# Turning a normalised activation by VectorE blocks and a DRAM round trip instead of by TensorE

## The reference

```python
x = x + tanh(g_xattn[0]) * L0_xattn(layernorm(x), ctx, ...)      # stage A
x = x + tanh(g_ffn[0])   * L0_ffn(layernorm(x), ...)             # stage F
x = x + tanh(g_xattn[1]) * L1_xattn(layernorm(x), ctx, mask)     # stage L
x = x + tanh(g_ffn[1])   * L1_ffn(layernorm(x), ...)             # stage M

def L0_ffn(x, proj1, proj1_bias, proj2, proj2_bias, gate_w):     # hidden size 2048
    h = gelu(x @ proj1.T + proj1_bias)
    return h @ proj2.T + proj2_bias
```

## Time and profile before

| | us |
|---|---|
| median of 3 runs | 1939.48 (1938.37 to 1940.64) |
| profiled execution, its time | 1941.13 |
| profiled execution, its span | 1939.3 |

### The profile page before, as it was taken

The page is one execution under the profiler, slowest core; times in us unless marked ns, Lnnn a source line. Parts: engine busy times, 40 slices in busy tenths (PEclk is TensorE's granted clock), DMA queues, the critical chain, the costliest instruction groups (busy, mean ns, idle before and its releaser), DMA issues.

```text
span 1939.3 us, 25583 instructions
## 1 busy us (share of the span) xinstructions
PE 1900.6 (98%) x10102; PEld 962.7 (50%) x10102; DVE 1035.4 (53%) x2260; ACT 559.7 (29%) x873; POOL 280.7 (14%) x277
## 2 busy tenths in 40 slices
PE   6999998999999999999999999999999999999999
PEld 4556555644444444444444444444544444444444
DVE  7688866764545453443535545554555555545422
ACT  3145423422222221112212233232222333333321
POOL 3023211111102010101100011111111111111111
PEclk9999998999999999999999999999999999999999
DMA  6013322220101111110101020101010101000000
GB/s 218 12 42 124 106 89 82 87 98 17 44 28 60 28 64 50 56 55 22 62 1 55 1 71 1 50 1 50 1 50 1 50 1 45 5 11 13 1 22 22
DMA packets 56041, 86.99 MB, mean 45 GB/s; under 512 B 9042, under 2 KB 17362, under 8 KB 55922
## 3 DMA queue, kind: packets, MB, share of 16 engines
q1 hardware_dynamic: 55922, 85.36, 13.8%
HBM read 60.17 MB, written 25.17 MB: 44 GB/s over the span
## 4 chain that ended last, share of the span: by engine, by line
PE 86%; issue 8%; DVE 3%; POOL 1%; DMA 1%; ACT 1%; POOLq 0%; SPq 0%; DVEq 0%
PE bank L835 44%; PE bank L939 16%; PE bank L1033 10%; PE bank L844 5%; PE bank L919 4%; PE bank L885 1%; PE bank L904 1%; POOL arena L802 1%; PE bank L1020 1%; PE bank L968 1%; PE bank L995 0%; DMA x_after_ffn<-arena 0%; PE bank L984 0%; PE bank L983 0%; DMA arena<-x_after_attention 0%
## 5 line engine op out<-in xcount | busy, mean ns | idle before, releaser
L835 PE MATMUL bank<-arena 128*128 128x512 f16 x4608 | 1043.4, 380 | 3.1 <-DVE arena L1286 2.3
L835 PEld LDWEIGHTS bank<-arena 128*128 128x128 f16 x4608 | 451.0, 98 | 522.7 <-issue 5.5
L939 PE MATMUL bank<-arena 128*128 128x512 f16 x1536 | 352.1, 379 | 1.2 <-DVE arena L1469 1.2
L1033 PE MATMUL bank<-arena 128*128 128x512 f16 x1152 | 264.3, 379 | 0.9 <-POOL arena L802 0.9
L1621 DVE SCALAR_TENSOR_TENSOR arena<-bank,arena 128x512 f32<-128x512 f32 x96 | 72.0, 750 | 332.1 <-PE bank L835 332.1
L939 PEld LDWEIGHTS bank<-arena 128*128 128x128 f16 x1536 | 150.1, 98 | 173.9 <-DVE arena L1469 1.7
L1467 DVE TENSOR_SCALAR arena<-arena 128x512 f16<-128x512 f32 x128 | 69.4, 543 | 305.4 <-ACT arena L1134 305.2
L1134 ACT ACTIVATE arena<-bank,arena 128x512 f32<-128x512 f32 x128 | 99.6, 778 | 457.3 <-PE bank L835 454.3
L802 POOL TENSOR_TENSOR arena<-arena 128x512 f16<-128x512 f32 x96 | 111.1, 1157 | 628.7 <-ACT arena L1171 628.7
L844 PE MATMUL bank<-arena 128*128 128x128 f32 x1012 | 150.1, 279 | 26.4 <-DVE arena L1234 14.1
L1033 PEld LDWEIGHTS bank<-arena 128*128 128x128 f16 x1152 | 112.1, 98 | 128.3 <-POOL arena L802 1.4
(11 more groups left out here) (173 smaller groups left out, 1221.9 us busy)
## 6 DMA issues: line engine op xcount, KB each, us to landing
arena<-in_L_ffn_proj SPq DMA_DIRECT2D x48, 256.0 KB, 2.9
x_after_attention<-arena SPq DMA_DIRECT2D x8, 1024.0 KB, 4.7
arena<-x_after_attention SPq DMA_DIRECT2D x8, 1024.0 KB, 5.6
x_after_ffn<-arena SPq DMA_DIRECT2D x8, 1024.0 KB, 4.5
arena<-x_after_ffn SPq DMA_DIRECT2D x8, 1024.0 KB, 6.2
arena<-in_x SPq DMA_DIRECT2D x7, 1024.0 KB, 5.4
out<-arena SPq DMA_DIRECT2D x7, 1024.0 KB, 4.2
arena<-in_L_ffn_down_proj SPq DMA_DIRECT2D x48, 96.0 KB, 2.0
```

The source lines that it names most:

```text
L835: m = e.matmul(bank[b][:, :], wT[l][:, c, tile * P:(tile + 1) * P], y[h][:, c, :], start=n == 0, stop=n == NPASS - 1)
L939: m = e.matmul(bank[t][:, :], hv[h][:, 0, t * P:(t + 1) * P], w2T[l][:, j, :], start=j == 0 and i == 0, stop=j == NH - 1 and i == 2)
L1033: m = e.matmul(bank[t][:, :], hv[h][:, 0, t * P:(t + 1) * P], dnT[l][:, j, :], start=j == 0 and i == 0, stop=j == NR - 1 and i == 2)
```

## The change

In stage F, for batches 1 to 7 (`in_blocks`), the turned x is made in another way. `norm` is as before. VectorE then turns each 32x32 block of the 128x512 tile in place (`block`, into one of two new buffers `yb_s`), and SyncE stores the result to DRAM (`bstore`, 256 KB). When all four are there, four DMAs (`bload`) read them back, one for each 32 rows of the target, into a new fp32 buffer `yraw` with features on partitions; the runs in memory are 32 elements (128 bytes). Then ScalarE copies `yraw` to the high half in four pieces (`whole`), and GpSimd subtracts for the low half. `up` waits for these instead of for the turns. The task list for such a batch is that of `block_tasks`. The buffers lie above the old arena, which grows from 207 to 219 KB per partition. The line with `rate` isn't in the diff. Below, the three parts behind the DMAs are of GpSimd's, ScalarE's and VectorE's programs, in this order.

```diff
+def in_blocks(i):
+    ph, b = i
+    return ph == "F" and b > 0
...
     def ln_tasks(i, apart=False):
+        if in_blocks(i):
+            return block_tasks(i)
...
+    def block_tasks(i):
+
+        def stats():
+            for t in range(NT):
+                add("stat", i, t)
+            add("rs", i)
+
+        def step(t):
+            if t < NT:
+                add("norm", i, t)
+            if t > 0:
+                add("block", i, t - 1)
+                add("bstore", i, t - 1)
+
+        def whole(c):
+            add("whole", i, c)
+        return ([stats] + [lambda t=t: step(t) for t in range(NT + 1)] + [lambda: add("bload", i)]
+                + [lambda: None] * 6 + [lambda c=c: whole(c) for c in range(NC)])
...
+            elif kind == "bstore":
+                _, i, t = step
+                m = nth[step]
+                k = (nth["bload", i] - 1) % 2
+                w.wait_ge(b_ok, m)
+                if nth["bload", i] > 2:
+                    w.wait_ge(b_in, 64 * (nth["bload", i] - 2))
+                e.dma_start(yscr[k, t * P:(t + 1) * P, :], yb_s[(m - 1) % 2]).then_inc(b_out[(m - 1) % 2], 16)
+            elif kind == "bload":
+                _, i = step
+                m = nth[step]
+                k = (m - 1) % 2
+                w.wait_ge(b_out[0], 32 * m)
+                w.wait_ge(b_out[1], 32 * m)
+                if m > 1:
+                    w.wait_ge(b_lo, NC * (m - 1))
+                for q in range(4):
+                    rows = slice(q * 32, (q + 1) * 32)
+                    e.dma_start(yraw[rows, :, :].rearrange("r c (a s) -> r c a s", s=32),
+                                yscr[k].rearrange("(a r) (c q s) -> q r c a s", r=32, c=NC, q=4)[q]).then_inc(b_in, 16)
...
+            elif kind == "whole":
+                _, i, c = step
+                w.wait_ge(b_hi, n)
+                y_free(w, i)
+                hi, lo = y_of(i)
+                e.tensor_tensor(lo[:, c, :], yraw[:, c, :], hi[:, c, :], ALU.subtract).then_inc(b_lo)
...
+            elif kind == "whole":
+                _, i, c = step
+                w.wait_ge(b_in, 64 * nth["bload", i])
+                y_free(w, i)
+                e.activation(y_of(i)[0][:, c, :], yraw[:, c, :], ACT.Copy).then_inc(b_hi)
...
+            elif kind == "block":
+                _, i, t = step
+                m = nth["norm", i, t]
+                w.wait_ge(yn_ok, m)
+                if n > 2:
+                    w.wait_ge(b_out[(n - 1) % 2], 16 * ((n - 1) // 2))
+                e.transpose(yb_s[(n - 1) % 2], yn_s[(m - 1) % 2]).then_inc(b_ok)
```

More of the change, by code:

```diff
@@ L371, in build @@
 def build(nc, x_in, ctx_in, mask_in, gx_in, gf_in, wq, wg, bg, wkv, wo, w1, b1, w2, b2,
-          gw, gup, dnp, mg, dom, xa, xb, out, stack):
+          gw, gup, dnp, mg, dom, xa, xb, yscr, out, stack):
     plan = make_plan()
@@ L375, in build @@
     KB = 256
-    arena = stack.enter_context(nc.sbuf_tensor("arena", [P, 207 * KB], F32))
+    arena = stack.enter_context(nc.sbuf_tensor("arena", [P, 219 * KB], F32))
     def at(kb, words, dt=F32):
@@ L410, in build @@
     yn_s = [at(168 + 2 * i, D) for i in range(2)]
+    yb_s = [at(207 + 2 * i, D) for i in range(2)]
+    yraw = at(207 + 4, NC * TOK).rearrange("p (c n) -> p c n", c=NC)
     h_s = [at(172 + 2 * i, TOK) for i in range(2)]
@@ L498, in build @@
     y_turned, y_hi, y_lo = sem("y_turned"), sem("y_hi"), sem("y_lo")
+    b_ok, b_in, b_hi, b_lo = sem("b_ok"), sem("b_in"), sem("b_hi"), sem("b_lo")
+    b_out = [sem(f"b_out{i}") for i in range(2)]
     w_chain, w_rec, w_mx, w_zero, w_scaled = (sem(n) for n in ("w_chain", "w_rec", "w_mx", "w_zero", "w_scaled"))
@@ L634, in build, with y_ready @@
         w_landed[w] = landed[w % 4]
-    def y_rank(i):
-        return nth["turn", i, NT - 1]
+    def y_ready(w, i):
+        if in_blocks(i):
+            w.wait_ge(b_lo, nth["whole", i, NC - 1])
+        else:
+            w.wait_ge(y_lo, nth["turn", i, NT - 1])
     def bcast(v):
@@ L850, in tensor_program @@
                 w.wait_ge(const, C_ID)
-                w.wait_ge(yn_ok, n)
-                turn4(step, yn_s[(n - 1) % 2], y_turned)
+                m = nth[("norm", *step[1:])]
+                w.wait_ge(yn_ok, m)
+                turn4(step, yn_s[(m - 1) % 2], y_turned)
             elif kind == "wturn":
@@ L863, in tensor_program @@
                 _, b, j = step
-                w.wait_ge(y_lo, y_rank(("A", b)))
+                y_ready(w, ("A", b))
                 w.wait_ge(w_lo, n_lo["q"])
@@ L923, in tensor_program @@
                 _, b, j = step
-                w.wait_ge(y_lo, y_rank(("F", b)))
+                y_ready(w, ("F", b))
                 w.wait_ge(w_lo, n_lo["1"])
@@ L961, in tensor_program @@
                 v = bank[k][:, 0:NT * CTX].rearrange("p (t s) -> p t s", t=NT)
-                w.wait_ge(y_lo, y_rank(("L", b)))
+                y_ready(w, ("L", b))
                 w.wait_ge(c_copied, 2 * n)
@@ L988, in tensor_program @@
                 v = bank[k][:, 0:NT * NE].rearrange("p (t s) -> p t s", t=NT)
-                w.wait_ge(y_lo, y_rank(("M", b)))
+                y_ready(w, ("M", b))
                 w.wait_ge(w_lo, n_lo["gw"])
@@ L1054, in y_free @@
             w.wait_ge(sc_mm, b + 1)
+    yn_read = {nth[step]: (b_ok, nth[("block", *step[1:])]) if in_blocks(step[1]) else (y_turned, nth[("turn", *step[1:])])
+               for step in plan.steps if step[0] == "norm"}
     def y_of(i):
@@ L1232, in vector_program @@
                 if n > 2:
-                    w.wait_ge(y_turned, n - 2)
+                    w.wait_ge(*yn_read[n - 2])
                 e.tensor_scalar(yn_s[(n - 1) % 2], x[:, t, :], mv[:, t, 0:1], rs[:, t:t + 1], ALU.subtract,
@@ L1660 @@
     from concourse.bass_utils import run_bass_kernel_spmd
-    nc = bacc.Bacc("TRN2", target_bir_lowering=False, num_devices=1)
+    nc = bacc.Bacc("TRN2", target_bir_lowering=False, num_devices=1, dynamic_dma_scratch_size=1024)
     arrays, args = {}, []
@@ L1671 @@
     xb = nc.dram_tensor("x_after_ffn", (NB, TOK, D), F32, kind="Internal").ap()
+    yscr = nc.dram_tensor("normalised_blocks", (2, TOK, D), F32, kind="Internal").ap()
     out = nc.dram_tensor("out", (NB, TOK, D), F32, kind="ExternalOutput").ap()
     with ExitStack() as stack:
-        build(nc, *args, xa, xb, out, stack)
+        build(nc, *args, xa, xb, yscr, out, stack)
     r = run_bass_kernel_spmd(nc, [arrays], core_ids=[0])
```

## The result

| | us |
|---|---|
| before, median of 4 runs | 1939.74 (1938.37 to 1940.64) |
| after, median of 4 runs | 1954.11 (1953.82 to 1954.86) |
| ratio, with its 95% interval | 1.0075 (1.0063 to 1.0087) |
| after, profiled execution: time, span | 1953.82, 1952.0 |

The change costs 14.4 us. The forecast was 13.2 us, and 1954.11 us lies inside its range of 1942 to 1962.

The account below looks back on a forecast made before the run. TensorE, busy 98% of the span, was taken as the bound. Turns -12.2, wait -0.3, net stall +23.4 and clock +2.3 gave +13.2 us: 1952.7 us, with an 8-in-10 range of 1942 to 1962.

Parts of the forecast that it names:

- The large term: Batch 7, `down` (7,1) to `up` (7,4): 19 leftover weight calls issued without matmuls, net stall 23.4 us.
- What the removed turns give: TensorE, feed-forward batches 1 to 7: 28 transpose groups, 12.2 us, and one 0.31 us wait go; gain 12.5 us.
- What hides the added work: Beside TensorE: VectorE's block transposes (0.6 us each) and GpSimd's subtractions (1.16 us) were to cost nothing.
- The DMAs: Block loads of 8192 128-byte pieces per batch: 6 to 20 us to landing, 10 taken, at no cost.
- rival 3: 128-byte loads come too late for `up` 11's GELU, deciding from 27 us (53 ns per packet); about 2050 us; chance 0.11.
- The size of the stretch: Before `up` (7,4): SyncE's 50 down_proj DMAs, then the router's weight, delay it by 29.2 us.
- SyncE never waits: In batch 7's stretch, staging buffers free up before SyncE's issues need them, with the scale at about +9 us.
- rival 1: Batch 7's stretch is bound by the engines, not SyncE's issues: 19.9 us, +3.9 in all, 1943.4 us; chance 0.10.
- The clock: Behind batch 7's stretch: 4.6 us of matmuls at half speed, 2.3 us more, bounds 0 and 5.
- The sum: Whole kernel: -12.2 - 0.3 + 23.4 + 2.3 = +13.2 us, to 1952.7 us.
- net stall: Batch 7, before `up` (7,4): 29.2 us later, less 5.8 us of transposing done elsewhere before, 23.4 us.

Follow-up runs that it names:

- e1: The changed kernel with the weight-conversion rate set for 18 slots per side list instead of 8: 1927.74 us.
- e2: The kernel before, without blocks, with only the weight-conversion rate lowered to about 0.187 of a call per slot: 1976.66 us.
- e8: e1 with the block loads cut into runs of 4 elements (16 bytes), 65536 packets per batch: 2113.06 us.
- e9: e1 without the six empty slots between block loads and ScalarE's copies, rate set for the shorter list: 1927.62 us.
- e7: e1 with the block loads cut into runs of 8 elements (32 bytes), 32768 packets per batch: 1942.46 us.
- e4: The changed kernel with GpSimd's two powers for down_proj's scale taken before the all-reduce instead of after it: 1956.00 us.
- e3: The changed kernel with each down_proj group loaded by one contiguous DMA instead of 3 or 4 (part of the output wrong): 1952.00 us.
- e5: e4 with one small idle GpSimd addition right behind the all-reduce of down_proj: 1953.92 us.
- e6: e5 with one DMA for each down_proj group, as in e3 (part of the output wrong): 1946.08 us.
- e10: e1 with stage A's all-reduce for proj2's maximum planned behind the same batch's `rs`, its followers later: 1918.42 us.

## Why the prediction was right, point by point

**The large term was the right one.** The forecast was a stretch between `down` (7, 1) and `up` (7, 4), because ten more slots of each side list leave 19 calls of `weights` undone. It is there, with 13 turns in it, SyncE issues through it, and half clock lies behind it. e1 removes it by the rate alone (-26.4 us), e2 makes it without the blocks. That is shown.

**What the removed turns give.** Predicted 12.5 us. e1 against before: 11.9, with the new wait of 1.45 in it.

**What hides the added work.** VectorE's transpose took 0.70 us (taken 0.6, bounds 0.54 and 1.5), GpSimd's subtraction 1.38 (taken 1.16). GpSimd's subtraction stretches VectorE's split from 0.75 to 1.74 us where they meet, as its bias did in the earlier trace rows. In the kernel after TensorE waits for none of them. Right, as nothing.

**The DMAs.** Taken 10 us to landing between 6 and 20; it was about 8. A packet took 12.9 ns, between my bounds of 7.6 (3.9 us for 8192 on 16 engines) and 36, and near the lower one. The condition of rival 3, 27 us, is what e8 measured (27.0), and e9 shows 7.2 us of ScalarE's wait in each batch that cost nothing. But 27 us is only the point for `down` 11: e7, with the data there after 25.45 us, loses time already, because the subtractions that come late slow VectorE down. I had asked only when the split of `up` 11 is wanted, and not what stands behind it. Rival 3's price, over 53 ns, is four times too high. The rule of the Trainium skill that I set beside it (VectorE: DVE Perf Modes, The three transpose paths: a plain strided DMA copy is 19 times slower than the crossbar's transpose when the innermost destination stride is large) is not tested by any run: none uses the crossbar, and the innermost elements are contiguous here. The estimate that I made from it, nineteen times a megabyte load, did not come true: 1 MB in runs of 128 bytes took about 8 us where a megabyte load took 5.6, and even in runs of 16 bytes, with 50 us, it is 9 times. One term here was wrong and hidden: SyncE takes 1.25 us (median of 28) for each `bload` DMA of 2048 packets, not 0.5.

**The size of the stretch.** Predicted 29.2 us, measured 32.06. Counted from the moment in which TensorE is free: the issue of the router's weight ends at +25.9 where +23.3 was predicted, 2.6 us late. Of this some 1.8 us is the start, since the issues begin 1.35 us before TensorE is free and not 3.2 (the load of x stands later against the projections than in the earlier trace rows), and 0.8 us the issues, 26.77 us for 50 instead of 26.0. Landing is 0.6 us quicker: the maximum at +27.5, against +25.5. The tail of small work behind it, 4.5 us instead of 3.7.

**The step that failed: "SyncE never waits".** It rested on a scale at about +9. VectorE's scale came at 1032.01, 16.1 us after TensorE was free, because GpSimd's arithmetic stands 7.2 us behind the all-reduce. SyncE's buffers come free later: 0.535 us an issue against 0.49 in e4. In the sum this is only some 2 us, because the two holds are side by side, as e3, e5 and e6 show; but it is why rival 1, in which fewer issues would have brought the stretch to 19.9 us, could not have come true by that alone. e3 is that case: 28.5 us. Only with the gap moved too, in e6, did it come down to 22.3. The row was there before I predicted: the second gap of GpSimd is what made the 9.90 us of the earlier trace rows, and I took that stall only as a measure for the clock. Nearer still, in the kernel before GpSimd's power for down_proj at 839.12 has 7.79 us of "issue" in front of it, at the very step that the stretch was to contain.

**The clock.** Predicted 2.3 us, measured 1.6 (`up` (7, 4), 4.16 instead of 2.59). Windows of the kernel after: within the stretch, and the first three microseconds behind it and the next three (start and end, length, busy us of PE, PEld, DVE, ACT and POOL, granted clock, DMA share, GB/s):

```profile
1021.00:1024.00 3.00, 0.48 (x3) 0.48 (x3) 2.11 (x6) 0.00 (x0) 0.38 (x1) 0.50 0.60 163
1048.00:1051.00 3.00, 3.00 (x9) 1.07 (x10) 2.67 (x8) 0.00 (x0) 0.00 (x0) 0.50 0.28 87
1051.00:1054.00 3.00, 3.00 (x15) 1.39 (x14) 1.54 (x5) 1.39 (x2) 1.04 (x1) 0.97 0.00 0
```

The granted clock is 0.50, the lower level of 1.2 GHz, from the end of a stop of 7.4 us on. It does not stay there throughout: after the sixteen transposes in a row at 1034.18 it is 0.74 in the three microseconds from 1036 and 0.83 in those from 1039, then 0.50 again from 1042 and through the first projection, and full in the second. In e5 and e6 it cost 0.9 and 1.4 us more behind stretches that were shorter, so its price is not told by the length of the stretch.

**The sum.** Turns and their wait -11.9 to -12.5 (predicted -12.5), net stall +26.2 (predicted +23.4), clock +1.6 (predicted +2.3); 15.3 to 15.9 by these terms. The spans differ by 12.7, and the medians by 14.4, 1 us less than the terms. The earlier start of stage F, 2.2 us in the profiled execution, would more than fill that; 1.7 of it is accounted for above, by the kernel's start and by GpSimd's gaps, which differ from run to run. So the total came out 1.2 us off where the stretch alone is 2.8 us off: part of that is luck.

## What to carry to other kernels

Where a list of steps is paced by the number of free slots, whoever adds tasks to it also moves what fills the remaining ones: count the slots up to the point that collects the rest, before and after, and set the rate with them; here that was worth 26 us against the 12 us for which the change was made. Before a stall is costed by the engine that looks slowest, look for a second hold beside it that ends nearly as late, since taking away either shows little. And look at an idle time marked "issue" on a side engine around a special instruction: here some 6 us came ahead of an all-reduce and some 7 behind it wherever arithmetic stood next to it, and they could be planned to where nobody waits.

## What the runs showed of the hardware

- GpSimd stands some 6 us ahead of a partition all-reduce (6.02 before 286.42 in e1, 6.00 before 289.31 in e10) and 6.7 to 7.8 us behind it, before its next arithmetic (7.42 before 294.22 in e1, 7.07 before 296.75 in e10, 7.17 before 1030.86 in the kernel after). A memset behind it is not held, and the gap begins only when the arithmetic instruction stands first: in e4 it follows the memset of 1037.90, 14 us after the all-reduce. Records MODIFY_POOL_CONFIG stand at its beginning, at 1023.6 in the kernel after and at 1038.4 in e4. What is done in it no run shows.
- The loads of the blocks passed 1310 to 1370 packets in a microsecond, whether these had 128, 32 or 16 bytes, so the number of packets told the time and not the bytes. The time that a packet took on its DMA engine was not the same: 12.9 ns at 128 bytes, 8.9 at 32 and at 16.
- SyncE took 0.49 us for each DMA of down_proj in e4, and 1.25 us (median; 0.59 to 2.84) for one that is cut into 2048 packets.
